# A common projection for q and k, a shorter seam between attention and routing, and expert units of one tile, in a kernel of attention and routed experts on one core

## The reference, cut to what matters

```
# 1. attention over the positions of each image
q = Wq x + bq;  k = Wk x + bk          # 32 rows each, from 256 channels
v = Wv x + bv                          # 256 rows
x = alpha * v softmax(q^T k)^T + x
# 2. proxy attention over normalised tokens, with a running sum
prods = proxy @ LN(t);  t = t + sum_p softmax(prods/4)_p * cumsum(prods_p * LN(t))
# 3. a mixture of 8 experts, two for each token
logits = LN(t) @ gate_w.T;  two largest, softmax of the two
t = t + sum_e share_e * (gelu(LN(t) @ w1[e] + b1[e]) @ w2[e] + b2[e])
```

## Time and profile before

| what | us |
|---|---|
| median of 3 runs | 783.26 |
| the profiled execution | 781.53 |
| its span, first to last instruction | 779.7 |
| TensorE busy in it | 713.2 |
| VectorE, GpSimd, ScalarE busy in it | 440.9, 407.9, 331.9 |

### The profile page before, as it was taken

The page is one execution under the profiler, slowest core; times in us unless marked ns, Lnnn a source line. Parts: engine busy times, 40 slices in busy tenths (PEclk is TensorE's granted clock), DMA queues, the critical chain, the costliest instruction groups (busy, mean ns, idle before and its releaser), DMA issues.

```text
span 779.7 us, 18458 instructions
## 1 busy us (share of the span) xinstructions
PE 713.2 (91%) x5438; PEld 676.9 (87%) x5439; DVE 440.9 (57%) x1047; ACT 331.9 (43%) x640; POOL 407.9 (52%) x480
## 2 busy tenths in 40 slices
PE   5899999999948888489999999999999999999993
PEld 4899898998926666389999999999999999999993
DVE  3675756756636999735445455455454454454551
ACT  2673755747515677332323323323323223233230
POOL 1474565787662443273555546546555555555233
PEclk9999999999969999599999999999999999999997
DMA  7759568497460333224557536665576276273122
GB/s 243 247 174 398 208 264 359 163 333 252 171 271 28 111 110 109 84 75 120 170 156 229 178 55 206 186 176 148 155 246 166 41 237 175 48 229 77 19 29 30
DMA packets 45873, 130.14 MB, mean 167 GB/s; under 512 B 5185, under 2 KB 35521, under 8 KB 41217
## 3 DMA queue, kind: packets, MB, share of 16 engines
q1 hardware_dynamic: 30560, 104.86, 36.3%
q0 software_dynamic: 13904, 19.45, 14.6%
q10 hardware_dynamic: 1360, 5.24, 1.7%
HBM read 186.80 MB, written 47.59 MB: 301 GB/s over the span
## 4 chain that ended last, share of the span: by engine, by line
PE 55%; issue 1%; DMA 0%; POOL 0%; DVE 0%; ACT 0%; POOLq 0%; DVEq 0%
PE ps_h L73 9%; PE ps_h L74 9%; PE ps_h L75 9%; PE ps_y L73 8%; PE ps_y L75 8%; PE ps_y L74 8%; PE ps_x L1596 2%; PE ps_y L1589 1%; DMA out_tok<-y,to_row 0%; POOL out_tok L1471 0%; DVE xtl L1531 0%; DVE yb L1551 0%; DVE y L1558 0%; ACT xth L1496 0%; POOL to_row L1467 0%
## 5 line engine op out<-in xcount | busy, mean ns | idle before, releaser
L1505 ACT ACTIVATE g<-ps_h,bias 128x256 f32<-128x256 f32 x288 | 120.8, 471 | 277.7 <-PE ps_h L75 277.7
L1471 POOL DMA_INDIRECT out_tok<-y,to_row x72 | 126.9, 1763 | 137.7 <-DVE y L1558 117.2
L73 PE MATMUL ps_h<-xth,wbuf 128*128 128x256 f32 x576 | 163.2, 283 | 3.3 <-issue 1.8
L73 PE MATMUL ps_y<-wbuf,gl 128*128 x576 | 164.6, 286 | 0.0
L74 PE MATMUL ps_h<-xtl,wbuf 128*128 128x256 f32 x576 | 163.1, 283 | 0.0
L75 PE MATMUL ps_h<-xth,wbuf 128*128 128x256 f32 x576 | 161.8, 281 | 0.0
L75 PE MATMUL ps_y<-wbuf,gh 128*128 x576 | 161.7, 281 | 0.0
L74 PE MATMUL ps_y<-wbuf,gh 128*128 x576 | 161.7, 281 | 0.0
L73 PEld LDWEIGHTS ps_h<-xth,wbuf 128*128 128x128 f32 x576 | 108.0, 188 | 3.7 <-issue 2.1
L75 PEld LDWEIGHTS ps_h<-xth,wbuf 128*128 128x128 f32 x576 | 109.6, 190 | 0.0
L74 PEld LDWEIGHTS ps_y<-wbuf,gh 128*128 128x128 f32 x576 | 108.8, 189 | 0.0
(11 more groups left out here) (239 smaller groups left out, 1284.9 us busy)
## 6 DMA issues: line engine op xcount, KB each, us to landing
wbuf<-wsplit SPq DMA_DIRECT2D x71, 2048.0 KB, 8.1
wsplit<-wbuf SPq DMA_DIRECT2D x14, 2048.0 KB, 11.9
wraw<-in_w SPq DMA_DIRECT2D x16, 1024.0 KB, 7.9
raw<-in_x_ch ACTq DMA_DIRECT2D x5, 1024.0 KB, 8.8
normed<-x SPq DMA_DIRECT2D x8, 528.0 KB, 3.0
tok<-in_x_tok SPq DMA_DIRECT2D x1, 4096.0 KB, 16.7
out_tok<-tok SPq DMA_DIRECT2D x8, 512.0 KB, 3.7
x_rows<-normed,from_row POOLq DMA_INDIRECT x72, 3.4
```

The source lines that it names most:

```text
L73: eng.matmul(out, ll, rh, start=first, stop=False)
L1471: pool.indirect_dma_start(out=out, out_offset=bass.IndirectOffsetOnAxis(ap=to_row[:, par, s:s + 1], axis=0), in_=y[:, par, s, :], in_offse ...
L1505: last = act.activation(g[:, f, :], ps_h[:, q, f % 2, :], ACT.Gelu_apprx_tanh, bias=bias1[:, bass.ds(e, 1), f:f + 1].rearrange("p a f -> p ...
```

## The change: what it does

1. **Common projection.** q and k come out of one projection: the weights are stacked as q, q, k, k in 128 columns, 12 matmuls in all at `it` 6, into `ps_sc`. ScalarE copies 64 rows of each (`high_qk`, two instructions) and then k's high rows twice more (`repeat_k`, two instructions of 32 rows); VectorE makes the two low parts and copies q's high rows once more (`repeat_q`). `score` waits for both. ScalarE's order at the end of an image changes with it.
2. **Splitting of weights.** GpSimd's instruction of 128x2048 is cut in four (`PIECES`). Of the very last chunk VectorE takes half (`last_weights`).
3. **Seam from stage A to stage B.** The wait for the stores goes to the start of stage B on SyncE. Stage B's first clearings come ahead of most `sem_inc`, under a semaphore of their own for `weight_t`. SyncE also stores the second layer of experts 0 and 1 (2 MB each).
4. **Units of one tile.** `make_table` counts pairs of tiles (256 rows) and an expert's odd tile apart. Of the 36 units, numbers 7, 15, 23 and 31 are now units of one tile (`alone`), with 128 rows in `layer1`, `layer2` and what lies between. Their weights have a buffer of their own (`lone_w`), which SyncE fills in four loads of 1 MB ahead of each. VectorE works out their table (`lone_table`) at the start of stage C. With more than 32 pairs or 4 odd tiles, a second part of 10 units of 256 rows runs. Gathers and scatters stay at two per unit.
5. **Program of stage C.** TensorE's units are all written out; the other engines' loops have eight units per turn. Row buffers of stage C lie in the room of the tokens.

```diff
-PAIRS = 2 * TOK // PAIR + E - 1
-USUAL = 2 * TOK // PAIR + E // 2
+PIECES = 4
+PERIOD = 8
+LONE = PERIOD - 1
+LONES = E // 2
+FULL = 2 * TOK // PAIR
+USUAL = FULL + LONES
+FULL_TOP = FULL + E - 2
+PAIRS = FULL_TOP + E
...
+            def high_qk(b):
+                act.wait_ge(qk_mm, done(b))
                 act.wait_ge(scored, done(b * IT - 1))
+                for kind in range(2):
+                    at = slice(kind * 2 * MID, (kind + 1) * 2 * MID)
+                    act.activation(qk3[at, kind], ps_sc[at, :], ACT.Identity, bias=bqk[at, 0:1]).then_inc(qk_hi, 1)
+            def repeat_k():
+                for row in range(2):
+                    last = act.activation(qk3[row * MID:(row + 1) * MID, 1], ps_sc[3 * MID:4 * MID, :], ACT.Identity,
+                                          bias=bqk[3 * MID:4 * MID, 0:1])
+                last.then_inc(k_rows, 1)
...
+                    if it == IT - 2 and more:
+                        hi_tile(it + 1)
+                        high_qk(b + 1)
+                        for n in (IT - 2, IT - 1):
+                            weights_high(n)
+                        repeat_k()
...
+            def repeat_q(b):
+                dve.tensor_copy(qk3[2 * MID:3 * MID, 0], qk3[0:MID, 0]).then_inc(q_rows, 1)
...
+                        m = n // PIECES
+                        for i in range(PIECES if more or (par, part) != (1, 1) else PIECES // 2):
+                            last = pool.tensor_tensor(wbuf[:, par, at + n + i * m:at + n + (i + 1) * m],
...
+                def last_weights(b):
+                    for n in (1, 2):
+                        tok.sums_of_weights(dve, *BATCHES[n], n)
+                    n = W2AT // 2
+                    dve.wait_ge(w_hi, (b * 4 + 4) * 2)
+                    dve.tensor_tensor(wbuf[:, 1, WROW - n // 2:WROW], wraw[:, 1, n // 2:n],
+                                      wbuf[:, 1, W2AT + n // 2:W2AT + n].bitcast(F32), ALU.subtract)
...
-                    if more and it >= IT - 2:
-                        project_qk(b + 1, it - (IT - 2))
+                    if more and it == IT - 2:
+                        project_qk(b + 1)
...
         @block.sync  # stage B
+            for par in range(2):
+                sp.wait_ge(w_out[par][0], 16 * (E // 2 + 1))
+                sp.wait_ge(w_out[par][1], 16 * (E // 2))
...
+            for e in range(2):
+                sp.dma_start(wsplit[e, :, W2AT:WROW], wbuf[:, e, W2AT:WROW].bitcast(F32)).then_inc(second_out, 16)
...
         # VectorE at the start of stage B
+            dve.memset(weight_t[:, 0], 0.0).then_inc(weight_zeroed, 1)
             dve.memset(prod[:, 0], 0.0).then_inc(zeroed, 1)
             dve.memset(state[:, 0], 0.0).then_inc(zeroed, 1)
+            for s in (attn_d, state_d, tok_d, stat2_d, mv2_d, raw_d, mg_d, logit_d, top_d, gap_d, topid_d, topf_d,
...
+            dve.memset(weight_t[:, 1], 0.0).then_inc(weight_zeroed, 1)
+            dve.memset(prod[:, 1], 0.0).then_inc(zeroed, 1)
...
         # stage C
+        def alone(u, at):
+            return at % PERIOD == LONE and not (isinstance(u, int) and u >= USUAL)
+        def rows_of(u, at):
+            return P if alone(u, at) else PAIR
...
+            def lone_weights(u, at):
+                layer, n = at // 2, W2AT // 2
+                e = entry(sp, T_EXPERT, u + (LONE - at), E - 1)
+                cols = slice(at * n, (at + 1) * n)
+                sp.dma_start(lone_w[:, cols].bitcast(F32),
+                             wsplit[bass.ds(e, 1)].rearrange("a p w -> (a p) w")[:, cols]).then_inc(lone_in[layer], 16)
...
+                    if at < 4 and not (isinstance(u, int) and u + LONE - at >= USUAL):
+                        lone_weights(u, at)
...
-                            last = mm3(pe, ps_h[:, q, f % 2, :], (wh[:, k, rows], wl[:, k, rows]),
-                                       (xth[:, par, k], xtl[:, par, k]), k == 0, k == KT - 1)
+                            last = mm3(pe, ps_h[:, q, f % 2, 0:n], (wh[:, k, rows], wl[:, k, rows]),
+                                       (xth[:, par, k, 0:n], xtl[:, par, k, 0:n]), k == 0, k == KT - 1)
...
-                for s in range(2):
+                for s in range(rows_of(u, at) // P):
                     rows = slice(s * P, (s + 1) * P)
                     for f in range(FT):
...
+                if lo == 0:
+                    lone_table()
+                x_low(lo, lo % PERIOD)
...
-                steps(pe, body, lo, hi, hi)
+                steps(pe, body, lo, hi, hi, written_out=True)
```

More of the change, by code:

```diff
@@ L547, in routing_weights @@
                         tok.largest(dve, *BATCHES[n], n)
-                    if not more and it == IT - 1:
-                        for n in (1, 2):
-                            tok.sums_of_weights(dve, *BATCHES[n], n)
+                def last_weights(b):
[5 more added lines that the diff above has]
+                                      wbuf[:, 1, W2AT + n // 2:W2AT + n].bitcast(F32), ALU.subtract)
                 full_v(0)
@@ L572, in image @@
                         wait_apart(dve, tok_in, 16)
-                    if more and it == IT - 1:
-                        low_qk(b + 1, 1)
+                    if more and it == IT - 2:
+                        for kind in range(2):
+                            low_qk(b + 1, kind)
+                        repeat_q(b + 1)
+                    if not more and it == IT - 1:
+                        last_weights(b)
                     dve.wait_ge(summed, done(g))
@@ L587, in _ @@
             low_qk(0, 1)
+            repeat_q(0)
             images(dve, image)
@@ L686, in image, with stage_b @@
                         turn(it + 1)
-                    if more and it >= IT - 2:
-                        project_qk(b + 1, it - (IT - 2))
+                    if more and it == IT - 2:
+                        project_qk(b + 1)
                     weigh(it)
-            project_qk(0, 0)
-            project_qk(0, 1)
+            project_qk(0)
             pe.wait_ge(wsm_ok, 2)
             images(pe, image)
-def stage_b(nc, sem, tok, wbuf, wsplit, ident, fixed, xn, tabs, bias1, bias2, records, normed, b1_t, b2, out):
+def stage_b(nc, sem, tok, w_out, wbuf, wsplit, ident, fixed, xn, tabs, bias1, bias2, records, count_i, n_pairs, ends,
+            expert, expert_id, normed, b1_t, b2, out):
     with ExitStack() as ctx:
@@ L1198, in decode @@
+                then(dve.tensor_copy(expert_i[:, :], expert[:, 0:REST]))
+                dve.tensor_scalar(tabs[:, T_BUFFER, 0:REST], expert_i[:, :], 1, None, ALU.bitwise_and)
+                then(dve.scalar_tensor_tensor(out=tabs[:, T_FIRST, 1:REST], in0=expert[:, 1:REST], scalar=float(E - 1),
+                                              in1=first[:, 1:REST], op0=ALU.is_lt, op1=ALU.mult))
             def decode():
@@ L1322, with stage_c @@
 T_EXPERT, T_COLUMN, T_FIRST, T_NEXT, T_BUFFER, T_TOTAL, T_CHANGED = range(7)
-def stage_c(nc, sem, wbuf, ident, tabs, bias1, bias2, records, wsplit, normed, out):
+def stage_c(nc, sem, room, wbuf, ident, tabs, bias1, bias2, records, count_i, n_pairs, ends, pair_experts, expert_id,
+            wsplit, normed, out):
     with ExitStack() as ctx:
@@ L1556, in result @@
                 dve.wait_ge(share_d, done(u))
-                for s in range(2):
+                for s in range(m):
                     last = dve.tensor_scalar(y[:, par, s, :], yb[:, s, :], share[:, slot, s:s + 1], None, ALU.mult)
```

416 lines of the change are left out of this document (250 added, 166 removed).

## The result

The changed kernel takes 760.2 us (median of 3 runs, 759.6 to 761.1) where the kernel before took 783.26: a ratio of 0.971, with a 95% interval from 0.969 to 0.973. A second series of five runs beside the experiments gave 758.8 us and 0.969 (0.968 to 0.971). The forecast was 756, with a range from 746 to 768. The profiled execution of the changed kernel took 760.2 us with a span of 758.5, against 781.53 and 779.7 before: 21.3 us, where the sum of the steps had said 27.0.

The account below looks back on a forecast made before the run. TensorE was taken to bound stages A and C, VectorE stage B. From 781.5 us, -8.3 - 1.0 + 0.6 - 3.1 - 0.5 + 0.4 - 15.1 = -27.0 gave 754.5; with 1.7 for the median, 756 us, range 746 to 768.

Parts of the forecast that it names:

- Seams between images: Stage A, three seams: 12 matmuls fewer on TensorE each, 2.78 us, with the new copies covered; -8.3 us.
- First projection: Start of stage A: projection ends 2.8 us earlier, score 1.0 earlier; -1.0 us, less certain if TensorE's clock falls.
- GpSimd in pieces: Stage A: each piece costs an extra start, felt only in the last image before ScalarE's load; +0.6 us (0 to 0.8).
- Seam A to B: End of stage A: without SyncE's store wait GpSimd ends last, VectorE's half chunk fits in idle time; -3.1 us (2.0 to 3.6).
- Seam B to C: Start of stage C: `lone_table` hidden in VectorE's idle time, `make_table` slightly longer; +0.4 us (0 to 1.6).
- Short units: Stage C, four one-tile units: half of layer 2, two transposes, layer 1 at 0.105 us per matmul; -15.1 us (12.3 to 23.1).
- Rival A: Short units' layer 1: weight loads hide, columns set the pace at 0.064 us per matmul; 23.1 us gained, 748 us; chance 0.20.
- Written out at no price: Stage C: writing out TensorE's units neither costs nor wins time, as TensorE has no wait at a loop's turn.
- Rival C: Stage C: TensorE's written-out program comes late by DMA; a loss from 0.96 us per unit, 812 us at 2; chance 0.06.
- The end of the program: Behind the last unit: tail and scatter taken to be as before, with no term in the sum.
- Rival B: Short units: a cover is missing and the clock falls, layer 2 costing 11.4 us more in all; 767 us; chance 0.11.
- Its bounds: Whole kernel: the forecast's own bounds, said to come from its terms, 750 to 763 us.

Follow-up runs that it names:

- two_projections: The changed kernel with the 12 matmuls of the common projection run twice, 24 in all, same result: 770.5 us, 0.985 of the kernel before.
- one_piece: The changed kernel with GpSimd's low halves in one instruction of 128x2048 again (128x1024 for the last chunk): 759.5 us, 0.971 of the kernel before.
- stage_a_wait: The changed kernel with SyncE's wait for the last stores back at the end of stage A: 761.5 us, 0.973 of the kernel before.
- half_columns: The changed kernel with layer 1 of the four short units streaming 64 columns in place of 128: 769.5 us, 0.983 of the kernel before.
- wait_last: The changed kernel with GpSimd waiting for its last scatters behind the branch around the second part, not ahead of it: 757.8 us, 0.967.
- short_second_part: The changed kernel with code for 3 units, not 10, in the second part that this input never runs: 758.0 us, 0.968.

## Why the prediction was right, and where it was not

- **Seams between images: right** in size and reason; two_projections turns the sum round.
- **First projection: the size by luck.** -0.8 of -1.0 came out of two things that were not in the sum. The score came 2.3 us earlier and not 1.0, and the clock that the prediction had feared took 1.5 back. The step that failed is "the projection ends 2.8 us earlier, near 17.9". It ended 4.4 us earlier: it began 1.1 us sooner (11.38, before 12.50), and most of its matmuls are 0.43 us apart and not 0.232, so 12 fewer save 3.3 us. ScalarE's first copy (before: the earlier trace rows, 20.68):

```profile
16.32 2.25 ACT L415 ACTIVATE qk<-ps_sc,bqk 64x1024 fp32r<-64x1024 f32 x2 [7.01 <-PE ps_sc L82]
```

  From there to the score the working holds, 4.6 us where it had 4.3. In ten profiles without filling the fall came in five, always with the first score at 20.4 to 20.9 us, never with it at 21.5 or later; TensorE had idled for 2.7 to 3.0 us in all of them. In the late ones but two_projections the first projection ran at the lower clock to its end or nearly so. What decides stays open.
- **GpSimd in pieces: the size was half of it and the reason wrong.** The prediction looked for the loss at the last load alone. It is 1.0 us ahead of it, as the experiment one_piece shows: a shorter image gives GpSimd less time for the same work, so its weights run into the next image's `vl`. With 12 more matmuls per image (two_projections, pieces as after) TensorE's long wait is gone (0.2 us) and the last image takes 35.45 us. Taking the pieces away doesn't bring the time back, since the load then ends last: the last image is bound by two things that stand close together.
- **Seam A to B: right**, -2.9 of -3.1. GpSimd ended last, as said, though VectorE's half of the chunk was not hidden as said: it took 2.20 us and pushed the last addition to 208.99. stage_a_wait shows that the wait made 2.1 us of it. The further half microsecond of stage B did not come.
- **Seam B to C: right side, nothing lost.** `lone_table` was covered.
- **Short units: the mechanism right, the term mis-sized.** "I take 0.105, the nearest rows" should have been 0.111; four units gave 13.9 and not 15.1 us. Rival A (loads hide, 0.064) falls by the 0.111 us, which half_columns has with 64 columns as with 128. The 81 ns that the Trainium skill, TensorE: Matmul & The Clock Gate, section Back-to-back issue gap, has for 128 columns with their load is not what these matmuls of `fp32r` weights take.
- **Written out at no price: right against the kernel before, wrong in its reason.** The prediction read from the loop of four that nothing is won by writing units out. For a loop of eight units, which the short units' period brings, each turn costs 6.65 us: without the writing-out the change would have kept some 10 of its 24 us. By the Trainium skill's rule (Runtime: NRT & Kernel Launch, Instruction fetch mechanics) a branch stalls where its target is not in what has been fetched; both loops agree. The loop of four fetched nothing while it turned, so its turns fall outside the rule, and it was wrong to count seven of them as stalls that the rule asks for. Rival C fell, though the written-out code does come in by DMA (32 packets from 320 to 760 us, before 10): the one wait named issue in stage C is 1.9 us after, as before.
- **The end of the program: missing.** The second part grew from 3 to 10 units and no step asked what is past it. It cost 2.5 us, by wait_last and short_second_part a fetch behind the last landing.
- **Rival B came in small**: 1.5 us at 336 to 340 us in the first profile, behind two idle stretches of TensorE (1.4 and 1.9 us) and not in the short units.
- **Its bounds.** "750 to 763" is not what its terms give: their ends added come to 746 and 767, nearly the whole range that it states.

Of the 5.7 us between -27.0 and -21.3, the end makes 2.5, the clock at the start of stage C 1.5, the short units 1.2, the last image 0.7; the rest is below what these executions repeat.

## What to carry to other kernels

Count the code that a branch jumps over, also code that never runs: if the branch stands behind the last wait, its fetch is on the path; put the branch ahead of the wait. Ask of a loop whether its code is fetched again at each turn; the instruction queue of the DMA view shows it. When units get shorter, ask which fixed cost per matmul is left (here 0.111 us for 128 columns and for 64), and read the granted clock there: with 64 columns it fell though the profile shows no gap. When a seam of one engine gets shorter, look at the engine that has the same work in less time, here GpSimd, and at the last load it releases.

## What the runs showed of the hardware

- Matmuls with a 128x128 load each and 128 or 64 moving columns come every 0.111 us; with 64 the granted clock halves in the course of the layer although TensorE shows no gap (half_columns).
- A loop of eight units stalls TensorE for 4.1 to 4.3 us per turn and fetches all the time, one of four neither stalls nor fetches (no packet of an instruction queue from 440 to 720 us).
- One pair of elementwise instructions on VectorE and GpSimd went slowly side by side: VectorE's half chunk of 128x1024 took 2.20 us (2.85 in one_piece) where its `xl` of that size takes 1.22; GpSimd's last three pieces took 4.75 us where four elsewhere take 5.04, so the one beside VectorE some 2.2 in place of 1.26. It is no rule for all pairs: VectorE's `ptl` of 128x1024 at 188.97 takes 1.20 amid GpSimd's four pieces of 5.04. What sets the pairs apart no run asked.
- Two executions of one kernel differ in whether the clock falls behind the same idle stretch of TensorE, 1.5 us at the start (0.8 net of an earlier score) and 1.5 us in stage C; losses of that size are read from events, not from medians.
